# One convolution tap moved to ScalarE and GpSimd, and a ScalarE copy placed ahead of a normalise

## The reference

```
# layer 0
h      = layernorm(x)                       # over 96 channels
p      = h @ w_in + b_in                    # 96 -> 192 channels
local  = depthwise 3x3 convolution of p     # 9 taps, one scale per channel and tap
mixed  = 0.25 * (four decaying scans of local, along rows and columns) + local
x      = x + layernorm(mixed) @ w_out + b_out
x      = x + gelu(layernorm(x) @ w1 + b1) @ w2 + b2      # 96 -> 384 -> 96
# layer 1
u, g   = layernorm(x) @ Wu + bu, sigmoid(layernorm(x) @ Wg + bg)
h      = 0;  8 times: h = g * (h @ A) + (1 - g) * u
x      = x + h
x      = x + gelu_tanh(layernorm(x) @ mlp_w1 + b) @ mlp_w2 + b
```

## Time and profile before

| | us |
|---|---|
| median of three runs | 229.38 |
| the profiled execution | 230.32 |
| its span (first to last instruction) | 228.4 |
| PE busy | 219.6 (96%) |
| VectorE busy | 182.7 (80%) |
| GpSimd busy | 148.8 (65%) |
| ScalarE busy | 137.0 (60%) |

### The profile page before, as it was taken

One profiled execution on the slowest core, in us unless ns is written; L12 is line 12 of the kernel. 1 busy time (PEld: TensorE's weight loads), 2 busy tenths in 40 slices (PEclk: granted clock), 3 DMA queues, 4 the chain that ended last, 5 costly groups with the idle time before them and its releaser, 6 DMA issues.

```text
span 228.4 us, 4138 instructions
## 1 busy us (share of the span) xinstructions
PE 219.6 (96%) x1332; PEld 182.3 (80%) x1332; DVE 182.7 (80%) x463; ACT 137.0 (60%) x308; POOL 148.8 (65%) x179
## 2 busy tenths in 40 slices
PE   8988896999999999999999999999999999999995
PEld 5676774889897989787888588888888878888885
DVE  7789999999999998996267987879696958667641
ACT  5765876768788675766563386636456552625262
POOL 7461877778979877949677573665849292836330
PEclk9999999999999999999999999999999999999999
DMA  3751000000000000000000003030313123021011
GB/s 110 214 178 54 1 0 0 4 0 0 3 0 1 3 1 0 3 0 0 0 3 0 1 36 106 34 105 0 117 58 118 56 83 93 34 70 37 0 40 63
DMA packets 11972, 9.30 MB, mean 41 GB/s; under 512 B 1232, under 2 KB 11696, under 8 KB 11952
## 3 DMA queue, kind: packets, MB, share of 16 engines
q1 hardware_dynamic: 11664, 8.97, 12.7%
q10 hardware_dynamic: 288, 0.09, 0.2%
HBM read 5.31 MB, written 3.74 MB: 40 GB/s over the span
## 4 chain that ended last, share of the span: by engine, by line
PE 80%; DVE 9%; DMA 4%; POOL 3%; issue 2%; SPq 1%; ACT 1%; DVEq 0%; POOLq 0%
PE bank L1410 12%; PE pA L1410 9%; PE pM L1361 8%; PE pM L1705 8%; PE bank L1535 7%; DMA x_all<-in_x 4%; DVE cA L1076 3%; PE bank L1578 2%; PE bank L1477 2%; PE bank L1583 2%; PE pA L1448 2%; PE bank L1680 2%; PE bank L1679 2%; PE bank L1685 2%; PE bank L1460 2%
## 5 line engine op out<-in xcount | busy, mean ns | idle before, releaser
L427 POOL TENSOR_TENSOR rs<-var,power 128x4 f32<-128x4 f32 x32 | 32.4, 1012 | 21.3 <-DVE var L967 18.2
L1076 DVE SCALAR_TENSOR_TENSOR cA<-pA,cols,cA 128x528 f32<-128x528 f32 x54 | 40.7, 754 | 0.2
L1361 PEld LDWEIGHTS pM<-w,hid 128*128 128x128 f32 x192 | 28.4, 191 | 5.7 <-issue 1.0
L1705 PEld LDWEIGHTS pM<-w,hid 128*128 128x128 f32 x168 | 26.9, 190 | 4.5
L1156 DVE SCALAR_TENSOR_TENSOR q<-th,bank 96x256 f32<-96x256 f32 x48 | 19.2, 412 | 13.3 <-PE bank L1410 13.3
L1361 PE MATMUL pM<-w,hid 128*128 128x96 f32 x192 | 28.9, 266 | 0.0
L1410 PE MATMUL pA<-q,a_half 96*96 96x256 f32 x96 | 27.0, 380 | 0.2 <-DVE q L1156 0.2
L1076 DVE SCALAR_TENSOR_TENSOR cB<-bank,cols,cB 128x256 f32<-128x256 f32 x56 | 26.4, 471 | 0.0
L1705 PE MATMUL pM<-w,hid 128*128 128x96 f32 x168 | 25.9, 266 | 0.0
L560 POOL TENSOR_TENSOR xl<-xt,xh 96x512 fp32r<-96x512 f32 x11 | 14.2, 1292 | 17.5 <-ACT xh L897 17.5
L1535 PE MATMUL bank<-local,mix 128*128 128x384 f32 x64 | 24.8, 497 | 0.1
(11 more groups left out here) (252 smaller groups left out, 612.7 us busy)
## 6 DMA issues: line engine op xcount, KB each, us to landing
moved<-blocks SPq DMA_DIRECT2D x11, 192.0 KB, 1.9
xt<-moved SPq DMA_DIRECT2D x33, 64.0 KB, 2.0
x_all<-in_x SPq DMA_DIRECT2D x8, 192.0 KB, 2.9
out<-y SPq DMA_DIRECT2D x7, 192.0 KB, 2.1
w<-in_w SPq DMA_DIRECT2D x1, 480.0 KB, 6.5
w<-in_w SPq DMA_DIRECT2D x1, 336.0 KB, 3.3
mix<-in_mix SPq DMA_DIRECT2D x1, 256.0 KB, 3.3
out<-y SPq DMA_DIRECT2D x2, 96.0 KB, 1.6
```

Source lines behind the costliest of these rows:

```text
L427: pool.tensor_tensor(rs[:, :], var[:, :], power[:, :], ALU.pow).then_inc(step, 1)
L1076: dve.scalar_tensor_tensor(out=acc, in0=src, scalar=col(f"k{'AB'[grp]}{k}"), in1=acc, op0=ALU.mult, op1=ALU.add).then_inc(s["conv_step"], 1)
L1361: last = pe.matmul(psum[:, k * D:(k + 1) * D], hid[:, j * TILE + k * P:j * TILE + (k + 1) * P], wc0("w2", j * D, (j + 1) * D), start=(j == ...
L1705: last = pe.matmul(dst, hid1[:, j * TILE + k * P:j * TILE + (k + 1) * P], wc1("m2", j * D, (j + 1) * D), start=j == 0 and (k == 0 if whole ...
```

## The change

For every tile but tile 0, tap 8 of the smaller group leaves VectorE. ScalarE writes the scaled shifted image to a new buffer `tap8` right behind tap 0 of the same tile, and GpSimd adds that buffer to `cB` between `rs2` and the normalise of its stage. Tap 1 of group B on VectorE now waits for that addition. VectorE's order changes at the start of a tile to A1, A2, (variance of tile n), B1, B2, and the end of `tap(8)` keeps only A8. The waits on B8 now name the last tap of group B by `conv_count`, which is B7.

In stage 2 alone, ScalarE's `normalize1` of tile 4 moves from ahead of the two copies of the mixed values to behind them.

```diff
@@ conv_count @@
-            return k if c == 0 else 16 * c - 8 + 2 * k - 1 + grp
+            order = {(1, 0): 1, (2, 0): 2, (1, 1): 3, (2, 1): 4, (8, 0): 15, (8, 1): 14}
+            return k if c == 0 else 15 * c - 7 + order.get((k, grp), 2 * k - 1 + grp)
@@ GpSimd, body0, behind rs2 @@
+                if tile_known(f) and not peeled(f, 0):
+                    pool.wait_ge(s["tap0_done"], 2 * f + 2)
+                    pool.wait_ge(s["tap8_made"], f)
+                    pool.tensor_tensor(cB[f % 2][:, :], cB[f % 2][:, :], tap8[:, :], ALU.add).then_inc(s["tap8_added"], 1)
+                if tile_known(m):
                     wait(pool, s["tr2_done"], m)
                     pool.wait_ge(s["ln2_step"], 2 * m + 2)
-                if tile_known(m):
                     normalize(xn2, x2, ng2, rs2, s["xn2_ready"])
@@ ScalarE, first_taps @@
+                    if grp == 1:
+                        wait(act, s["tap8_added"], f - 1)
+                        act.activation(tap8[:, :].rearrange("c (r w) -> c r w", w=SIDE), tap_views(f, 8)[1][1], ACT.Copy,
+                                       scale=col("kB8")).then_inc(s["tap8_made"], 1)
@@ ScalarE, body0 @@
-                if i >= 2:
+                if i >= 3:
                     normalize1(n)
...
                                        ACT.Copy).then_inc(s["mixed_ready"], 1)
+                if peeled(i, 2):
+                    normalize1(n)
@@ VectorE, tap and body0 @@
                             dve.wait_ge(s["tap0_done"], 2 * c + 1 + grp)
+                            if grp == 1:
+                                dve.wait_ge(s["tap8_added"], c)
...
-                    ln1_stats(lambda grp: tap(1, [grp]))
+                    ln1_stats(lambda at: tap(1 + at, [0]))
                 else:
-                    tap(1)
-                tap(2)
+                    tap(1, [0])
+                    tap(2, [0])
+                if peeled(c, 0):
+                    tap(2)
+                else:
+                    tap(1, [1])
+                    tap(2, [1])
...
-                    tap(8)
+                    tap(8, [0])
```

More of the change, by code:

```diff
@@ L186, in build @@
         cB = [sb(f"cB{k}", TOKENS) for k in range(2)]
+        tap8 = sb("tap8", TOKENS)
         local = sb("local", 2 * 2 * INNER)
@@ L213, in build @@
             "x_even_loaded", "x_odd_loaded", "bn1_step", "var1_ready", "ln1_step", "xn1_ready", "trx_done", "x1_split", "x1_lo",
-            "p_psum", "tap0_done", "conv_step", "cT_done", "local_ready", "mix_done", "mixed_ready",
+            "p_psum", "tap8_made", "tap8_added", "tap0_done", "conv_step", "cT_done", "local_ready", "mix_done", "mixed_ready",
             "bnm_step", "varm_ready", "lnm_step", "mtr_done", "mc_ready", "wout_done", "xb_ready", "x2_ready",
@@ L1371, in ln3_transposes @@
                     if peeled(f, 0):
-                        pe.wait_ge(s["conv_step"], conv_count(TILES - 1, 8, 1))
+                        pe.wait_ge(s["conv_step"], conv_count(TILES - 1, 8, 0))
                     elif peeled(f, 1):
```

## The result

The changed kernel took 232.16 us (median of 20 executions, 229.78 to 233.26), the kernel before, on the same chips, 229.74 (20 executions, 229.25 to 231.03). The ratio is 1.0072 with a 95% interval of 1.0051 to 1.0093: slower by 0.7%, and the median lies above the range of 229.1 to 230.9; the two medians by themselves are 1.05% apart. (A ratio leaves out executions that took over 1.5% more than the fastest of their kernel: two of 233.26 us here, and in the experiments one of e1, two of e6, one of e9 and three of e11.)

A forecast was written before the change was run, and what follows sets the result against it. It took PE as the bound (busy 96%), with VectorE setting the pace only where it ends last, as in stage 2. Stages 2, 4 and 6 cost 0.16 + 0.30 + 0.19 = 0.65 us on 229.38: 230.0 us, range 229.1 to 230.9.

The forecast's parts named there:

- 0.96 us of idle time that A8 ended: Stage 2, ahead of the `w_in_a(3)` load: PE idle 0.96 us until A8, so a shorter VectorE run would move PE.
- So the removal is worth nothing where PE is fed: B8 leaving VectorE: `w_in_a` waits for A8, ahead of B8, and `x2` has other waits; gain 0, at most 0.39 us.
- B: Rival: GpSimd's addition takes 1.00 us instead of 0.73 and the chain behind it shifts; 230.84 us, chance 0.19.
- Stage 2, 0.16 us: B1 of tile 2 waits for GpSimd's addition until 32.52, VectorE ready at 32.36; `w_in_a(3)` starts 0.16 us later.
- Stage 1, 0: Removing B8 gains nothing in stage 1, since `x2` behind it waits for `rsm`, 0.55 us late.
- Stage 4, 0.30: The addition delays the mixed copy, VectorE's statistics and A8; with no slack PE loses 0.30 us.
- The chain: GpSimd's addition, normalise and `rs1`, then ScalarE's normalise and mixed copy, then VectorE's statistics: normalise 0.50 us later, statistics 0.31.
- the wait of the statistics: Sign in the profile after: in stage 4 VectorE's statistics wait near 0.3 us for the mixed copy.
- Stages 3, 5 and 6: Stage 3 has 0.27 us free, stage 5's delays run side by side: 0 each; stage 6 loses 0.19 after B1 waits 0.77.
- The reorder at nothing: ScalarE's stage 2 reorder: worth nothing alone; with the addition it avoids a 0.1 us wait of the statistics.
- A8 alone ends stage 2: In stage 2 the end of A8 alone releases the `w_in_a(3)` load, 0.06 us later; B8 stands behind A8.

The follow-up runs named there:

- e1: The changed kernel run again with nothing else altered: median 230.76 us, ratio 1.0039 to the kernel before.
- e6: The change for tiles 1 and 2 alone, with the ScalarE reorder, other tiles as in the kernel before: 230.88 us, ratio 1.0060.
- e9: The change for tile 1 alone, with the ScalarE reorder, other tiles as in the kernel before: 229.56 us, ratio 0.9996.
- e11: The changed kernel with three more VectorE statistics instructions in stage 2, results unused: 234.22 us, ratio 1.0133.
- e5: The changed kernel with four unread matmuls of ones in TensorE's stage 2 wait, ahead of tile 3's projection: 230.40 us, ratio 1.0023.
- e13: The kernel before with only the change's VectorE order (A1, A2, variance, B1, B2), no tap moved and no addition: 230.40 us, ratio 1.0035.
- e2: The kernel before run again, unchanged, with a second profile: 229.56 us, ratio 0.9990.
- e17: The changed kernel with alternating A and B taps restored behind A2, and A8 ahead of B7: 229.65 us, ratio 1.0000.
- e4: The kernel before with only the ScalarE reorder of stage 2: 229.37 us, ratio 0.9991.
- e12: The kernel before with A8 of tile 2 placed ahead of B7 on VectorE: 230.09 us, ratio 1.0023.
- e14: The kernel before, in tile 2 tap 8 of B on ScalarE, added by GpSimd behind B7, A8 ahead of B7, ScalarE reordered: 230.02 us, ratio 1.0012.
- e3: The changed kernel without the ScalarE reorder, `normalize1` of stage 2 left where it was: 231.02 us, ratio 1.0040.
- e16: The kernel before plus the reorder, ScalarE's `tap8` and a GpSimd addition into an unread buffer, VectorE as before: 230.35 us, ratio 1.0007.

## Why the prediction was wrong

*The time: a missing cost.* The step that failed is the one that put TensorE's idle time, and with it its clock, at nothing: the sum has no term for the granted clock. TensorE's wait ahead of `w_in_a(3)` was read as "0.96 us of idle time that A8 ended", and only its end was followed; "So the removal is worth nothing where PE is fed" took no account of where the idle time goes. What the runs showed in its place: taking B8 of tile 1 away moved TensorE's 0.81 us of early idle time into stage 2, and with 0.35 more on VectorE that made 2.6 us of idle time where there had been 1.7. In 19 of 32 executions of the change the granted clock fell, which cost 2.1 us at 0.993 (e1: 232.24 against 230.14), and with the gap filled it fell in none of 12 (e5). None of the rivals has it; B, the one on the slow side, priced a dearer addition, which was 0.72 to 0.73 as taken.

*The time at full clock.* The six executions at full clock have a median of 230.03, the forecast to the hundredth, and that is luck. The forecast added 0.65 to 229.38, a median of three runs, where twenty runs of before gave 229.74; the difference measured at full clock is 0.29 (0.24 in e1 against the 229.90 beside it). The traces have 0.71 from the load of tile 2 to that of tile 7, near the 0.65, but they compare one execution of each kernel, and the spans of before at full clock range from 226.9 to 229.2 us.

*Stage 2, 0.16 us.* The forecast wait of B1 for the addition did not occur. `x2` to the addition's end is 3.79 (30.96 less 27.17), as forecast (32.42 less 28.62 is 3.80); but VectorE itself arrived later, at 3.93, since the sum counted A1 to A2 as 0.68, the step from A8 to B8, which belongs to two accumulators. Here A1 to A2 was 0.86 to 0.87. From `x2` to load the stage cost 0.34 to 0.39, and e13 shows 0.36 for the order alone.

*Stage 1, 0.* The cover that was named, `rsm` 0.55 late, was a matter of that profiled execution. In e2 `x2` follows at 1.70 behind the load of tile 2, in the change at 1.51, so 0.19 came back. With it the two stages cost 0.15 (13.50 against 13.35): right beside the 0.16, but by luck: two errors of opposite sign.

*Stage 4, 0.30: measured 0.34, stall 0.31.* The chain was late as written: ScalarE's normalise at 58.66 had waited 0.46 for `rs1`. But VectorE did not wait for the copy, it was itself 0.3 late by tap order and came to the statistics at 60.26 just as the copy was done. So the wait of the statistics that the prediction named as a sign did not appear. Two causes of one size lay side by side; e13 has the order without the addition (0.40, some 0.1 of it from a longer variance), e17 the chain (0.31 behind a wait of 0.44).

*Stages 3, 5 and 6.* 0 was forecast in stages 3 and 5, and -0.06 and -0.01 were measured. Stage 6: 0.19 forecast, 0.29 measured; B1 waited 0.58 instead of 0.77, again because A2 ended later, and B1 to B2 took its 0.12 behind it. The reorder at nothing: right (e4).

*A8 alone ends stage 2:* incomplete. Had B8 been the last thing ahead of `w_in_a`, the gain would still have been small, since `x2` binds just behind (e12, e14).

## What to carry to other kernels

Removing an instruction that an idle engine waited for also moves that engine's idle time: follow where TensorE's idle stretches land, how much lies close together and how long the longest is, since they can cost more through its clock than their own length. Filling the gap prevented it here (e5). Take the step between two instructions from a row where they stand to each other as they will, above all on whether the second reads what the first writes. And take slack from more than one profiled execution.

## What the runs showed of the hardware

- At the same kernel the granted clock fell in some executions and not in others (14 of 20, then 5 of 12), each time with the same order of work. It cost 2.1 us of 230 in e1, several times the change's cost at full clock (0.24 to 0.29 by the medians, 0.71 in the trace), and 1.4 us in e3.
- In e11 the clock fell inside a wait of TensorE of 2.58 us, some 0.6 us ahead of its end (an estimate from 0.87 in the stretch from 39 to 40 us), and was at 0.50 for 6 us of full work behind it.
- Two VectorE taps on the same accumulator back to back: 1.62 us for the pair of 128 x 528 and 0.99 for the pair of 128 x 256, against 1.43 and 0.86 for steps of 0.68 and 0.39 between different accumulators.
- A GpSimd addition of 128 x 256 took 0.72 to 0.73 us where it reads two buffers, and 0.61 in e16, where both inputs are the same buffer.
